# A fused Mamba-and-FFN block: one output product in three 16-bit terms, the input norm in place, and another order at the batch boundary

## The reference, cut to what matters

```python
def layer(x):
    x = x + layernorm(attn(layernorm(x)))
    return x + layernorm(ffn(layernorm(x)))

def attn(u):                       # heads 8, head width 64, state 64, inner width 512
    x, z = u @ Wx.T, u @ Wz.T
    x = silu(causal_conv4(x))
    b, c, dt = x @ Wb.T, x @ Wc.T, softplus(x @ Wdt.T + b_dt)
    y = ssd_scan(x, b, c, dt, -exp(log_a)) + d_param * x
    yn = group_norm_over_time_and_head_width(y) * gn_w + gn_b
    return (yn * silu(z)) @ Wout.T

def ffn(u):                        # hidden 1024, weights alpha * sign(w)
    return gelu(u @ bw1.T + b1) @ bw2.T + b2
```

## Time and profile before

| | |
|---|---|
| time, median of 3 runs | 1347.39 us (1345.3 to 1349.34) |
| the profiled execution: its time | 1347.9 us |
| its span, first to last instruction | 1346.2 us |
| mean granted TensorE clock | 0.982 of full |
| busy: PE, DVE, ACT, POOL | 94%, 78%, 56%, 36% |
| DMA | 32.89 MB, 7.3% of 16 engines |

### The profile page before, as it was taken

One profiled execution on the slowest core, in us unless ns is written; L12 is line 12 of the kernel. 1 busy time (PEld: TensorE's weight loads), 2 busy tenths in 40 slices (PEclk: granted clock), 3 DMA queues, 4 the chain that ended last, 5 costly groups with the idle time before them and its releaser, 6 DMA issues.

```text
span 1346.2 us, 27890 instructions
## 1 busy us (share of the span) xinstructions
PE 1265.5 (94%) x10616; PEld 809.9 (60%) x10616; DVE 1055.1 (78%) x2462; ACT 750.2 (56%) x1270; POOL 485.2 (36%) x559
## 2 busy tenths in 40 slices
PE   6899999999999999999999999999999999999676
PEld 3564657565575756656575665757567565766554
DVE  5574797879888797878978788887978789786575
ACT  5554574556745485554745567454755547455321
POOL 2030444224351434325433243514443154332633
PEclk9998999999999999999999999999999999999788
DMA  7010000101000010101001010010101000010100
GB/s 224 1 49 1 17 0 2 48 1 48 1 22 27 2 48 1 48 1 44 6 1 48 1 48 1 17 32 2 48 1 48 1 30 4 1 33 1 33 1 31
DMA packets 30564, 32.89 MB, mean 24 GB/s; under 512 B 1856, under 2 KB 28628, under 8 KB 30432
## 3 DMA queue, kind: packets, MB, share of 16 engines
q1 hardware_dynamic: 30432, 31.11, 7.3%
HBM read 22.72 MB, written 8.39 MB: 23 GB/s over the span
## 4 chain that ended last, share of the span: by engine, by line
PE 69%; DVE 19%; issue 5%; POOL 4%; ACT 2%; POOLq 0%; DVEq 0%; ACTq 0%
PE bank L1425 25%; PE bank L1619 8%; PE bank L1606 7%; PE bank L1537 5%; PE bank L1591 4%; DVE xs L1067 4%; PE bank L1515 4%; PE bank L1573 3%; PE bank L1560 2%; PE bank L1551 2%; PE bank L1507 2%; DVE un L1042 2%; PE bank L1435 2%; DVE gn_stats L1203 1%; DVE sh L1072 1%
## 5 line engine op out<-in xcount | busy, mean ns | idle before, releaser
L790 POOL TENSOR_TENSOR Cd<-Cd,CT 128x512 f32<-128x512 f32 x64 | 81.4, 1271 | 366.2 <-ACT Cd L987 366.0
L1425 PE MATMUL bank<-sh,WbT 128*128 128x512 f16 x768 | 177.1, 387 | 10.5 <-DVE sh L1072 10.5
L1425 PE MATMUL bank<-sh,WcT 128*128 128x512 f16 x768 | 175.9, 379 | 0.0
L1067 DVE SCALAR_TENSOR_TENSOR xs<-xi,vectors,xs 128x512 f32<-128x512 f32 x192 | 152.5, 803 | 7.7 <-ACT xs L893 3.4
L1425 PEld LDWEIGHTS bank<-sh,WbT 128*128 128x128 f16 x768 | 74.2, 99 | 101.7 <-issue 15.0
L1591 PE MATMUL bank<-WoutT,yT 128*128 128x256 f32 x512 | 118.5, 389 | 12.6 <-POOL yT L767 6.5
L977 ACT ACTIVATE mt<-bank 128x512 f32<-128x512 f32 x128 | 69.6, 600 | 108.1 <-PE bank L1507 108.1
L1425 PEld LDWEIGHTS bank<-sh,WcT 128*128 128x128 f16 x768 | 75.2, 98 | 86.5
L1606 PE MATMUL bank<-uh,sign1T 128*128 128x512 f16 x512 | 121.5, 383 | 2.0 <-DVE uh L1268 2.0
L1619 PE MATMUL bank<-sign2T,hh 128*128 128x256 f16 x1024 | 120.3, 277 | 1.8 <-DVE hh L1279 1.8
L1009 ACT ACTIVATE hf<-bank,vectors,alpha 128x512 f32<-128x512 f32 x128 | 99.5, 777 | 37.9 <-PE bank L1606 26.4
(11 more groups left out here) (196 smaller groups left out, 2453.5 us busy)
## 6 DMA issues: line engine op xcount, KB each, us to landing
xt<-L_attn_input_tensor_dram SPq DMA_DIRECT2D x16, 512.0 KB, 5.0
u<-L_attn_input_tensor_dram SPq DMA_DIRECT2D x16, 512.0 KB, 4.0
out_dram<-u SPq DMA_DIRECT2D x16, 512.0 KB, 3.0
yT<-in_L_ffn_w_dram SPq DMA_DIRECT2D x2, 512.0 KB, 9.7
u<-in_L_ffn_w_dram SPq DMA_DIRECT2D x2, 512.0 KB, 9.5
BT<-in_L_attn_Wx_dram SPq DMA_DIRECT2D x1, 512.0 KB, 4.8
BT<-in_L_attn_Wz_dram SPq DMA_DIRECT2D x1, 512.0 KB, 5.7
zs<-in_L_attn_Wb_dram SPq DMA_DIRECT2D x1, 512.0 KB, 5.3
```

Of the source, the lines that this page charges most:

```text
L790: pool.tensor_tensor(Cd[n % 2][:, :, :], Cd[n % 2][:, :, :], CT[:, :, q * P:(q + 1) * P], ALU.mult)\
L1067: nc.vector.scalar_tensor_tensor(out=xs[:, c, :], in0=xi[:, c, k:k + BLK], scalar=taps[:, c, k:k + 1], in1=xs[:, c, :], op0=ALU.mult, op1= ...
L1425: mm = nc.tensor.matmul(bank(t, key)[:, :], w[i][:, k, cols(m)], v[h][:, k, :], start=(a == 0), stop=(a == len(terms) - 1))
```

## The change

- **Output product of block 1.** `WoutT` is kept in float32 and, split at set-up, as `WoutT_parts` in float16 (ACT and DVE, two passes more each). A new step `gated` splits the gated `yT` of block 1: ACT writes the high half (`gated_high`), DVE the low half (`gated_low`) into `yg`, which lies in the upper half of the FFN's `hh`. It stands at the end of block 0 of the next batch, two slices behind each half of the end norm. `attention_out` of block 1 then makes 12 float16 instructions per chunk, 48 in all, in place of 32; the mid norm's eps is scaled to match. Block 0 stays in float32.
- **Input norm in place.** `xn` is gone; L1042 writes `xt`. `load_x` now waits for the transposes of `xt` (a bank's semaphore, from PE) instead of `xn_made`, the first one too.
- **Order at the ends of blocks.** `end_stat` goes ahead of the scores of chunk 2, the group norm's first statistics behind `back` 1, the end norm is cut in two, and the silu table load goes ahead of the second `xT`. In the first batch the input norm goes behind `back` 0.
- **Order at the batch boundary.** `gn_mean` goes ahead of the fourth `xi`; the convolution of slice 0 with its silu and split go ahead of the group norm's root; both gate parts of block 0 are DVE's; part 1 stands behind the convolution of slice 2.

```diff
             def load_x(t, j):
-                sp.wait_ge(*xn_made.count(t.ago(1), (j + 1) * NQ))
+                sp.wait_ge(*full(t.ago(1), ("xT", j, KD - 1)))
...
-            steps += tail(("head_stat", NJ - 1, 1), ("gn_sum",)) + own(("xi", 0, 3), ("silu_table",))
-            steps += tail(("gn_mean",), ("gn_root",)) + own(("conv", 0, 0, 0, 2), ("z", 0, 0)) + tail(("gn_fold",))
-            steps += own(("conv", 0, 0, 2, 3), ("z", 0, 1)) + tail(("gate", 0, 0)) + own(("z", 0, 2), ("z", 0, 3))
-            steps += own(("conv", 0, 1)) + tail(("gate", 0, 1)) + own(*[("z_in", 0, c) for c in range(KI)])
...
+            steps += own(("xi", 0, 0), ("xi", 0, 1), ("xi", 0, 2)) + tail(("head_stat", NJ - 1, 1), ("gn_sum",), ("gn_mean",))
+            steps += own(("xi", 0, 3), ("conv", 0, 0), ("silu", 0, 0), ("xs_hi", 0, 0)) + tail(("gn_root",))
+            steps += own(("conv", 0, 1, 0, 2), ("z", 0, 0)) + tail(("gn_fold",)) + own(("conv", 0, 1, 2, 3), ("z", 0, 1))
+            steps += tail(("gate", 0, 0)) + own(("xs", 0, 0), ("silu", 0, 1), ("xs_hi", 0, 1), ("conv", 0, 2))
+            steps += own(("z", 0, 2), ("z", 0, 3)) + tail(("gate", 0, 1)) + own(("xs", 0, 1), ("conv", 0, 3))
...
+        norm = [(who, "in_norm", nj)]
+        steps += own(("carry", j, 0), ("ends", j, 1)) + (own(("back", j, 0)) + norm if first else norm + tail(("O", j, 1)) + own(("back", j, 0)))
+        steps += own(("front", j, 2)) + tail(("end_stat", j))
+        steps += own(("score", j, 2), ("carry", j, 1), ("ends", j, 2)) + tail(("end_root", j)) + own(("back", j, 1), ("head_stat", j, 0))
+        steps += own(("front", j, 3), ("score", j, 3)) + [(who, "xT", nj, 0)] + tail(("end_norm", j, 0))
+        steps += tail(("gated", 1, 0)) if j == 0 else []
+        steps += own(("carry", j, 2), ("ends", j, 3), ("back", j, 2)) + [(who, "silu_table"), (who, "xT", nj, 1)] + tail(("end_norm", j, 1))
+        steps += tail(("gated", 1, 1)) if j == 0 else []
+        steps += own(("carry", j, 3), ("back", j, 3))
...
+    steps += [("Wo", 0, 0), ("Wo", 0, 1), ("mid_stat", 0), ("gated", 1, 0), ("gated", 1, 1), ("mid_norm", 0), ("ff_stat", 0), ("ff_norm", 0)]
...
+        yg = [[v[:, j * KI:(j + 1) * KI, :] for v in hh] for j in range(NJ)]
...
+            def gated_low(t, j, m):
+                for c in range(2 * m, 2 * m + 2 if j else 0):
+                    dve.wait_ge(*yg_hi.count(t, c + 1))
+                    nc.vector.scalar_tensor_tensor(out=yg[j][1][:, c, :], in0=yT[:, c, BLK:T], scalar=SY, in1=yg[j][0][:, c, :],
+                                                   op0=ALU.mult, op1=ALU.subtract).then_inc(yg_lo.sem, 1)
...
             def attention_out(t, j, m):
-                pe.wait_ge(*(g_late.count(t, gated * KI) if gated else g_out.count(t, KI)))
+                pe.wait_ge(*(yg_lo.count(t, KI) if j else g_out.count(t, (m + 1) * KI)))
+                for i in (2 * m, 2 * m + 1) if j else ():
+                    terms = [(c, w, v) for c in range(KI) for w, v in ((0, 0), (1, 0), (0, 1))]
+                    for a, (c, w, v) in enumerate(terms):
+                        mm = nc.tensor.matmul(bank(t, key)[:, (i % 2) * D:(i % 2 + 1) * D], yg[j][v][:, c, cols(i)],
+                                              WoutT_parts[w][:, c, :], start=(a == 0), stop=(a == len(terms) - 1))
```

More of the change, by code:

```diff
@@ L33 @@
 SG = 64.0
+SY = 16.0
 DECAY_FLOOR = -110.0
@@ L213, in turn_steps @@
         steps += own(("score", j, 1))
-        steps += own(("carry", j, 0), ("ends", j, 1)) + [(who, "in_norm", nj)] + tail(("O", j, 1)) + own(("back", j, 0), ("front", j, 2), ("score", j, 2))
-        steps += own(("carry", j, 1), ("ends", j, 2), ("back", j, 1)) + tail(("end_stat", j)) + own(("front", j, 3), ("score", j, 3))
-        steps += [(who, "xT", nj, 0)] + own(("carry", j, 2), ("ends", j, 3), ("back", j, 2)) + [(who, "xT", nj, 1)]
-        steps += tail(("end_root", j), ("end_norm", j)) + own(("carry", j, 3), ("back", j, 3), ("head_stat", j, 0))
+        norm = [(who, "in_norm", nj)]
[7 more added lines that the diff above has]
+        steps += own(("carry", j, 3), ("back", j, 3))
         if j == 0:
@@ L278, in mamba_sandwich_kernel @@
         WoutT = sb("WoutT", [P, KI, D])
+        WoutT_parts = [sb(f"WoutT{i}", [P, KI, D], F16) for i in range(2)]
         sign1T = sb("sign1T", [P, KD, FF], F16)
@@ L763, in gate @@
                 n = 2 * j + m
-                for c in range(KI if n else 0):
+                for c in range(KI if j else 0):
                     at = slice(n * BLK // 2, (n + 1) * BLK // 2)
@@ L853, in weights @@
                     elif name == "Wout":
-                        nc.scalar.activation(WoutT[:, 2 * k:2 * k + 2, :], w.rearrange("p (k n) -> p k n", k=2), ACT.Copy)\
-                            .then_inc(act_set, 1)
+                        w = w.rearrange("p (k n) -> p k n", k=2)
+                        nc.scalar.activation(WoutT[:, 2 * k:2 * k + 2, :], w, ACT.Copy).then_inc(act_set, 1)
+                        nc.scalar.activation(WoutT_parts[0][:, 2 * k:2 * k + 2, :], w, ACT.Copy, scale=SW).then_inc(w_split, 1)
                     elif name == "w2":
@@ L996, in head_normalise, with gated_high @@
                                          scale=gn_scale[:, c:c + 1]).then_inc(yn_out.sem, 1)
+            def gated_high(t, j, m):
+                s, sj = (t, 0) if ring_of(t, ("O", 0, 0)) is not final else (t.ago(1), NJ - 1)
+                act.wait_ge(*full(s, ("O", sj, NQ // 2 - 1)))
+                for c in range(2 * m, 2 * m + 2 if j else 0):
+                    act.wait_ge(*g_late.count(t, KI + c + 1))
+                    nc.scalar.activation(yg[j][0][:, c, :], yT[:, c, BLK:T], ACT.Copy, scale=SY).then_inc(yg_hi.sem, 1)
             def middle_high(t, j):
@@ L1307, in weights @@
                         dst, w = [v[:, :, :] for v in WdtT], w[:, 0:KI * HEADS].rearrange("p (k h) -> p k h", k=KI)
+                    elif name == "Wout":
+                        dve.wait_ge(act_set, k + 1)
+                        dst, w = [v[:, 2 * k:2 * k + 2, :] for v in WoutT_parts], w.rearrange("p (k n) -> p k n", k=2)
                     else:
```

75 lines of the change are left out of this document (37 added, 38 removed).

## The result

The changed kernel takes 1351.15 us (median of 12 runs, 1347.66 to 1351.98) against 1347.07 (12 runs, 1345.3 to 1349.34) of the kernel before beside it: ratio 1.0025, 95% interval 1.0016 to 1.0034. The forecast was 1338.4, range 1331 to 1345.

A forecast was written before the change was run, and what follows sets the result against it. PE, busy 94% of the span, was taken as the bound, DVE costing time only where PE waits. Block 0's end -1.4, boundary -6.0, load +2.8, first batch -3.5, tail -1.0: -9.1 from 1347.4, 1338.4 us; range 1331 to 1345.

The forecast's parts named there:

- The product: Block 1's output product: 48 float16 instructions in 5.5 us replace 32 in 7.07, so PE has 1.6 us less per batch.
- Two low halves 1.2: End of block 0: two low halves ahead of chunk 2's state sum cost DVE 1.2 us, 0.62 each.
- Rival 2: Contention: low halves beside POOL's product Cd take 0.15 us more each, +2.1 us in all, 1340.5; chance 0.14.
- The wait's place: PE's last state product of block 0 waits 1.4 us for DVE's yT sum, leaving 0.2 us gain a batch.
- nothing more is late: Behind PE's wait at block 0's end, the product's 1.6 us before B absorb the delay of DVE's convolutions.
- Rival 4: PE's clock falls after new waits, at block 0's end or the boundary: 2.0 us a batch, 14 more, 1352.4; chance 0.07.
- single waits of 1.60 and 1.92: First batch: these PE waits are followed by transposes of 0.66 us, as fast as any, arguing against a clock fall.
- The order at the end of block 0: Chunk 2's mt is late by 1.1 us; part of the 1.4 us wait comes early, with no extra cost.
- the sum is the same: Block 0's end: part of PE's 1.4 us wait moves earlier, to chunk 3's seg and transposes, without changing its total.
- The boundary: Between batches: both gates as late as before, but splits and following norms earlier; 0.85 us each, 6.0 in seven.
- First batch, tail: First batch loses PE's waits of 1.60 and 1.92, -3.5 us; the tail gains 1 us, between -3 and +1.
- The load: Start: SP's first load waits for a bank's semaphore until 4.8 us, delaying everything by 2.8, between 2.2 and 3.5.

The follow-up runs named there:

- order_before: f32_product with the kernel before's order at the ends of both blocks, boundary and input norm still changed; 1346.81 us.
- f32_product: Changed kernel with block 1's output product in float32 again and no gated halves, the rest as changed; 1341.91 us.
- no_low: Changed kernel with the low halves written for only 8 of 512 columns, the 48-instruction product kept; 1334.06 us.
- low_first: Changed kernel with the first two low halves ahead of the first half of the end norm; 1349.45 us.
- stats_behind: Changed kernel with the end norm's statistics behind the scores of chunk 2 instead of ahead of them; 1358.6 us.
- best1: Changed kernel with the halves made mid-block 0, block 1's product ahead of z, old order at both block ends, first load without a wait; 1333.75 us.
- best2: Changed kernel: halves made mid-block 0, product ahead of z, block 0's end in old order, first load free, tail halves before mid norm's statistics; 1321.57 us.
- hybrid_f32: f32_product with the old order at the end of block 0 and the changed order at the end of block 1; 1338.16 us.

## Why the forecast was wrong, step by step

One batch, each term as a difference of stretches between kernels. The terms sum to +1.0, with the halves at the mean of their two values; measured is 6.41 / 6 = +1.07, and the forecast was -1.05. Of the 2.1 between them the halves are 1.4 and the order at the end of block 0 is 0.9; the other terms nearly cancel:

| term | from | measured | forecast |
|---|---|---|---|
| boundary's order, with the input norm in place | A: order_before - before | -1.44 | -0.85 |
| order at the end of block 0 | A: f32_product - order_before | +0.91 | 0 |
| order at block 1's end, B's part of the boundary | B: f32_product - before | +0.38 | within the -0.85 |
| three-term product | B: no_low - f32_product | -1.67 | -1.6 |
| the halves | A: changed - f32_product | +3.29 or +2.36 | +1.4 |

- **The product: right** (-1.67).
- **"Two low halves 1.2": the step that failed.** They took 2.35. The price came from `sh` splits beside a still POOL, though the text itself named `Cd` as their neighbour. Rival 2 had the mechanism and a price of 0.15 for each half, from the convolutions beside POOL's gates; it is 0.5 on average and 1.07 at most. That price was a misreading of a merged row: of the nine convolution instructions that the earlier trace rows shows as 8.30 us, POOL's gates cover four. The trace of the kernel before, asked for narrower windows, has them apart:

```profile
484.58 4.50 DVE L1067 SCALAR_TENSOR_TENSOR xs<-xi,vectors,xs 128x512 f32<-128x512 f32 x4
...
489.12 2.99 DVE L1067 SCALAR_TENSOR_TENSOR xs<-xi,vectors,xs 128x512 f32<-128x512 f32 x4
```

These are 1.1 us each beside the gates and 0.75 behind them, so 0.4 more beside POOL and not 0.15, and three of them take 3.4 us there where the prediction has 2.8.

The Trainium skill (SBUF — State Buffer, the section SBUF: two separate sides) is stricter than the price I took: of a DVE instruction with two SBUF inputs and a GpSimd one that reads SBUF, the second to start is blocked until the first has ended. By that rule, the trace agrees at `Cd`: 550.28 + 1.30 + 0.68 = 552.26 as the end of a low half that starts at 550.37, and its 1.75 us end it at 552.12.

- **The wait's place: right; its size and what follows: wrong.** 1.81 + 0.68 against 1.4. Then the clock (four batches, 1.45 each) or a wait of 0.53 for DVE's state sum (three), behind the second pair, for which the forecast had only "nothing more is late". Rival 4 had 0.07, as a case apart; but it hangs on the length of the forecast's own wait: behind 0.76 us (no_low) the clock never fell, behind 1.70 (low_first) in three batches of seven, behind 1.81 in four (changed) and in five (stats_behind). The argument against it, single waits of 1.60 and 1.92 without a fall, was from two waits of the first batch.
- **The order at the end of block 0: overlooked.** I let the late scores of chunk 2 cost 0.35 in block 1 and nothing in block 0, as "the sum is the same". The wait is 0.68 to 0.83, 14 times (the fifteenth, 0.42 in the first batch, the kernel before has too), and in A the order costs 0.91 a batch.
- **The boundary: right in kind, too small.** A gains 1.44: besides the splits and `un`, the wait for the second gate fell from 0.93 to 0.46, where the forecast left it. But it needs the early moments of the new block end: with the old one B loses 1.68 (order_before), so with that block end it comes to +0.24 a batch.
- **First batch, tail: right as sums,** the first batch partly by luck. Its waits of 1.60 and 1.92 did go, as forecast. Then two stretches of low clock changed and nearly cancel: the products from 40.11 to 49.83, behind a wait of 1.94, take 9.72 us where the kernel before takes 7.41, and those from 109.97 to 122.85, again behind 1.94, take 12.88 where it takes 14.87 (granted clock from 30 to 60 us 0.83 for 0.94, from 100 to 140 us 0.96 for 0.87). **The load:** 3.5 for 2.8, at the bound that was named, since SP issued it at 5.47 and not at 4.8.

Of the two theories for f32_product and no_low, neither was right as a whole. Shown by runs: each term of the table as a difference of stretches, the price of low halves beside POOL and away from it, and that their place decides about the change. Not shown: why the clock falls behind one wait of 1.81 and not behind the next; and what sets it in the first 60 us. No run changes POOL's work alone; that POOL is what lengthens the low halves rests on the rows, in which all of best1's 32, away from POOL, take 682 to 686 ns.

## What to carry to other kernels

Price a moved or added instruction by rows of the same form **with the same neighbour on the other engine**: a low half, a VectorE instruction that reads two operands from SBUF (the on-chip memory), took 1.1 to 1.76 us beside GpSimd work, and 0.68 beside a still GpSimd. A merged row hides this: ask for the instructions that really lie beside the neighbour. Work that makes another engine faster belongs where its own engine waits: the same four halves cost 2.4 to 3.3 us a batch at the end of a block, and among the hidden slices 0.3 (best2's 155.04 a batch against hybrid_f32's 156.42 less the product's 1.67). Parts of a change may only work together, so give every end of a block or a boundary its own stretch of time, and compare stretches, not totals.
